# A two-layer decoder in one kernel: keys and values of twelve more items made at the head of the last phase, and two phases in another order of pieces

## The reference, cut to what matters

```
x = x + L0_attn(layernorm(x))            # causal attention over sines and cosines
x = x + L0_xattn(layernorm(x), ctx_768)  # attention to a context of 192 features
x = x + L0_ffn(layernorm(x))             # 16 experts, one per token, fixed capacity
x = x + L1_attn(layernorm(x))            # attention across the batch axis
x = x + L1_xattn(layernorm(x), ctx_768)
x = x + L1_ffn(layernorm(x))             # gated, operands quantised to four bits
```

```
q = einsum('sbd,ed->sbe', x, Wq);  k = einsum('sbd,ed->sbe', x, Wk)
align = softmax(tanh(einsum('sbd,tbd->bst', q, k) / sqrt(256)))
out = einsum('bst,tbd->sbd', align, x)
```

```
q = x @ Wq;  k = ctx @ Wk;  v = ctx @ Wv        # 16 heads of 16 features
out = softmax(q k^T / 4) v;  return out @ Wo
```

## Time and profile before

| | us |
|---|---|
| median of 3 runs | 3186.0 |
| lowest, highest | 3185.05, 3187.09 |
| profiled execution, its own time | 3185.23 |
| span of its trace | 3183.5 |
| TensorE busy | 3009.7 (95%) |
| VectorE busy | 2357.7 (74%) |
| ScalarE busy | 1802.2 (57%) |
| GpSimd busy | 1276.7 (40%) |
| batch attention, projections of steps 1 to 15 | 1813.47 to 1938.63 |
| last phase, first to last query projection | 1964.30 to 3064.42 |

### The profile page before, as it was taken

How to read it: one execution, slowest core, us unless ns; L and a number is a source line. 1 busy time by engine, 2 the same in 40 slices (tenths; PEclk the granted TensorE clock), 3 DMA queues, 4 the chain that set the end, 5 groups by cost and what they waited for, 6 DMA issues and landing times. The chain is left out here.

```text
span 3183.5 us, 57497 instructions
## 1 busy us (share of the span) xinstructions
PE 3009.7 (95%) x21110; PEld 2118.6 (67%) x21110; DVE 2357.7 (74%) x4842; ACT 1802.2 (57%) x3262; POOL 1276.7 (40%) x1927
## 2 busy tenths in 40 slices
PE   5899999999999999899999896799999999999998
PEld 3677777777777767566666563466666777777776
DVE  4799999999999986242111495689899888888886
ACT  5788888888888873111111232456556555555553
POOL 5466666666666652100000352233334333333332
PEclk7999999999999999899999998899999999999999
DMA  8888777778777774533334254534443434433330
GB/s 154 150 116 121 115 108 115 115 115 121 114 107 115 110 101 121 176 124 124 104 103 151 73 179 104 87 64 73 80 83 62 69 59 69 67 61 59 60 50 21
DMA packets 298345, 318.34 MB, mean 100 GB/s; under 512 B 35958, under 2 KB 279526, under 8 KB 298064
## 3 DMA queue, kind: packets, MB, share of 16 engines
q1 hardware_dynamic: 283664, 290.60, 51.1%
q0 software_dynamic: 6144, 15.68, 1.5%
q10 hardware_dynamic: 8256, 8.39, 0.8%
HBM read 104.31 MB, written 58.79 MB: 51 GB/s over the span
## 5 line engine op out<-in xcount | busy, mean ns | idle before, releaser
L629 DVE TENSOR_REDUCE xa_mx<-bank 128x2 f32<-128x512 f32 x1024 | 660.9, 687 | 147.9 <-PE bank L619 145.0
L733 ACT ACTIVATE xa_p<-bank 128x512 f32<-128x512 f32 x1024 | 569.7, 597 | 271.1 <-PE bank L723 268.9
L744 DVE SCALAR_TENSOR_TENSOR xa_p<-xa_p,bank 128x1024 f32<-128x1024 f32 x256 | 301.4, 1217 | 24.2 <-PE bank L712 13.8
L2204 POOL DMA_INDIRECT sa_y<-expert_out,sa_s x64 | 68.2, 1066 | 525.1 <-DMA expert_out<-ex_y 481.6
L756 PE MATMUL bank<-xa_p,xa_v 128*32 128x256 f32 x4096 | 272.9, 391 | 0.3 <-ACT ra_ot L1150 0.3
L1088 ACT ACTIVATE xa_p<-bank 128x384 f32<-128x384 f32 x512 | 235.9, 499 | 65.1 <-PE bank L1076 62.7
L1980 ACT ACTIVATE ex_h<-bank,ex_b 128x512 f32<-128x512 f32 x64 | 44.0, 687 | 362.3 <-PE bank L1969 362.3
L1097 POOL TENSOR_SCALAR_AFFINE_SELECT xa_p<-xa_p 128x256 f32<-128x256 f32 x512 | 199.2, 407 | 83.4 <-ACT xa_p L1088 82.8
L1999 PE MATMUL bank<-ex_w,ex_h 128*128 128x256 f32 x1024 | 224.8, 380 | 1.2 <-issue 0.9
L1969 PE MATMUL bank<-ex_xt,ex_w 128*128 128x512 f32 x512 | 224.0, 596 | 0.7 <-ACT ex_xt L1960 0.7
L619 PE MATMUL bank<-xa_ks,ex_w 96*128 96x256 bf16 x1024 | 197.3, 280 | 17.3 <-DMA ex_w<-xa_pq 14.3
(11 more groups left out here) (308 smaller groups left out, 6774.9 us busy)
## 6 DMA issues: line engine op xcount, KB each, us to landing
ex_w<-ra_parts SPq DMA_DIRECT2D x384, 128.0 KB, 4.6
xa_ks<-xa_pk SPq DMA_DIRECT2D x384, 128.0 KB, 4.6
ex_w<-in_L_ffn_W SPq DMA_DIRECT2D x32, 1024.0 KB, 6.9
xa_qs<-xa_pq SPq DMA_DIRECT2D x192, 128.0 KB, 4.7
ex_w<-xa_pq SPq DMA_DIRECT2D x192, 128.0 KB, 4.5
ra_x<-in_x SPq DMA_DIRECT2D x32, 256.0 KB
xa_ctx<-in_ctx_t SPq DMA_DIRECT2D x64, 128.0 KB, 2.2
queue<-zeros ACTq DMA_DIRECT2D x4, 2048.0 KB, 11.8
```

Of the source, the lines that this page charges most:

```text
L629: c.nc.vector.tensor_reduce(c.xa.row_max[:, :, n], halves(c.banks[2 + n % 2]), AX.X, ALU.max).then_inc(s.max_taken, 1)
L733: c.nc.scalar.activation(c.xa.p_beside[:, n // 2 % 4, :, n % 2, :], halves(c.banks[n % 2]), ACT.Exp, scale=SCALE).then_inc(s.exp, 1)
L744: c.nc.vector.scalar_tensor_tensor(out=p, in0=p, scalar=1.0, in1=c.banks[bank][:, :].unsqueeze(1).broadcast_to([P, TC, 2 * S]), op0=ALU.mi ...
```

## The change

A constant LATE = 12 is added. For items 16 to 27 of the last phase, TensorE makes keys in bank 7 and values in bank 5 in the phase's first four periods (`pe_late_keys`, `pe_late_values`), ScalarE copies both to a `keeps` tile (`act_late_keys`, `act_late_values`), SyncE stores the tile, and the item reads them back as the first sixteen do. The load waits for the store. Only items 28 to 31 still make keys and values in their own periods.

```
-AHEAD = 16
+AHEAD, LATE = 16, 12
 def was_ahead(b):
-    return B <= b < B + AHEAD
+    return B <= b < B + AHEAD + LATE

+def pe_late_keys(c, bank, b):
+    s = c.xa.s
+    c.pe.wait_ge(s.ctx_in[b % 2], 32 * (b // 2 + 1))
+    c.pe.wait_ge(*c.bank_out[bank])
+    side_matmuls(c, bank, c.wx.Wk, c.xa.ctx[b % 2]).then_inc(s.k_made, 1)
+    c.bank_out[bank] = (s.k_copied, b - B + 1)
+def pe_late_values(c, bank, b):
...
+    token_matmuls(c, bank, c.xa.ctx[b % 2], c.wx.Wv).then_inc(s.v_made, 1)
+    c.bank_out[bank] = (s.v_copied, b - B + 1)
+def act_late_keys(c, bank, b):
+    s, par = c.xa.s, b % 2
+    c.act.wait_ge(s.k_made, b + 1)
+    c.act.wait_ge(s.kept_out[par], 16 * ((b - B) // 2))
+    c.nc.scalar.activation(c.xa.keeps[par][:, 0], c.banks[bank][:, :], ACT.Copy).then_inc(s.k_copied, 1)
...
 def sp_xa_kept(c, kept, b):
...
+    c.sp.wait_ge(s.kept_out[par], 16 * ((b - B) // 2 + 1))
     for n in range(2):
         c.nc.sync.dma_start(c.xa.kept[par][n], kept[b - B][:, n]).then_inc(s.kept_in[par], 16)

 def pe_phase_e(c):
...
-        for b, _ in due(n, period, (27,), first=AHEAD):
+        for b in at(n, (401, 403, 745, 873, 961, 1209, 1337, 1394, 1609, 1785, 1817, 1865), B + AHEAD):
+            pe_late_keys(c, 7, b)
+        for b, _ in due(n, period, (216,), first=AHEAD + LATE):
             pe_xa_keys(c, 7, c.wx, B + b)
...
 def phase_e(c, d):
...
+    c.xa.keeps = [c.sb(f"xa1_keep{n}", [P, 2, KC * S]) for n in range(2)]
```

More of the change, by code:

```diff
@@ L2393, in pe_phase_d @@
     pe_d_first_turn(c)
-    for n in range((STEPS_D - 1) * period + 48):
-        for b, k in due(n, period, (27, 28), STEPS_D, first=1):
+    for n in range((STEPS_D - 1) * period + 29):
+        for b, k in due(n, period, (7, 8), STEPS_D, first=1):
             pe_d_turn(c, b, k)
-        for b, k in due(n, period, (30, 31), STEPS_D):
+        for b, k in due(n, period, (11, 12), STEPS_D):
             pe_d_project(c, b, k)
-        for b, _ in due(n, period, (34,), STEPS_D):
+        for b, _ in due(n, period, (15,), STEPS_D):
             pe_d_score(c, b)
-        for b, k in due(n, period, (41, 42, 44, 47), STEPS_D):
+        for b, k in due(n, period, (22, 23, 27, 28), STEPS_D):
             pe_d_sum(c, b, k)
@@ L2439, in pool_phase_d @@
     period = ROUND_D["pool"]
-    for n in range((STEPS_D - 1) * period + 6):
-        for b, _ in due(n, period, (2,), STEPS_D, first=2):
+    for n in range((STEPS_D - 1) * period + 5):
+        for b, _ in due(n, period, (1,), STEPS_D, first=2):
             pool_d_gather(c, d["expert_out"], b)
-        for b, _ in due(n, period, (5,), STEPS_D, first=1):
+        for b, _ in due(n, period, (4,), STEPS_D, first=1):
             pool_d_power(c, b)
@@ L2450, in sp_phase_d @@
     sp_xa_kept(c, d["kept"], B)
-    for n in range((STEPS_D - 1) * period + 10):
-        for b, _ in due(n, period, (0,), STEPS_D):
+    for n in range((STEPS_D - 1) * period + 19):
+        for b, _ in due(n, period, (1,), STEPS_D):
             sp_d_next(c, d, b)
-        for b, _ in due(n, period, (9,), STEPS_D):
+        for b, _ in due(n, period, (18,), STEPS_D):
             sp_d_out(c, out_rows[b], b)
@@ L2762, in pe_phase_e @@
             pe_e_turn_hidden(c, 2 + k % 2, b, k)
-        for b, _ in due(n, period, (299,), B - 1):
+        for b, _ in due(n, period, (2336,), B - 1):
             pe_e_down(c, 7, b)
@@ L2813, in act_phase_e @@
     period = ROUND_E["act"]
-    for n in range((B - 1) * period + 156):
-        for b, _ in due(n, period, (4,), first=1):
+    for n in range((B - 1) * period + 1449):
+        for b in at(n, (305, 355, 537, 641, 689, 809, 913, 969, 1097, 1137, 1145, 1425), B + AHEAD):
+            act_late_keys(c, 7, b)
+        for b in at(n, (353, 354, 593, 625, 713, 865, 897, 961, 1017, 1146, 1185, 1249), B + AHEAD):
+            act_late_values(c, 5, b)
+        for b, _ in due(n, period, (248,), first=1):
@@ L2816, in act_phase_e @@
             act_xa_high_k(c, 7, c.wx, B + b)
-        for b, _ in due(n, period, (6,), first=1):
+        for b, _ in due(n, period, (264,), first=1):
             act_xa_middle_k(c, B + b)
-        for b, _ in due(n, period, (5,)):
+        for b, _ in due(n, period, (240,)):
             act_xa_xn_t(c, 6, B + b)
-        for b, _ in due(n, period, (9,)):
+        for b, _ in due(n, period, (280,)):
             act_xa_high_q(c, 6, c.wx, B + b)
-        for b, _ in due(n, period, (13,)):
+        for b, _ in due(n, period, (304,)):
@@ L2824, in act_phase_e @@
             act_xa_middle_q(c, B + b)
-        for b, _ in due(n, period, (17,), first=1):
+        for b, _ in due(n, period, (352,), first=1):
             act_xa_values(c, 7, B + b)
-        for b, _ in due(n, period, (48,)):
+        for b, _ in due(n, period, (592,)):
             act_xa_rows(c, 2, 1, B + b)
-        for b, k in due(n, period, (54, 55, 56, 57, 58, 59, 60, 61, 63, 64, 66, 67, 68, 69, 70, 71)):
+        for b, k in due(n, period, (640, 648, 656, 664, 680, 688, 696, 704, 712, 720, 736, 744, 752, 760, 768, 776)):
```

153 lines of the change are left out of this document (84 added, 69 removed).

## The result

The changed kernel takes 3137.71 us (median of 4 runs, 3137.54 to 3137.85), the kernel before 3185.99 us (4 runs). The ratio is 0.9848, 95% interval 0.9836 to 0.9861: 48.3 us less, where 44 (3142) were forecast and 3128 to 3162 given.

The account below looks back on a forecast made before the run. TensorE was taken to bound steady periods, waits and lower clock the head, TensorE and VectorE batch attention. Terms -37.6 + 4.0 - 7 - 2 = -42.6 from 3185.23 us gave 3142.6, stated as 3142, range 3128 to 3162.

Parts of the forecast that it names:

- Term 1: Last phase: items 16 to 27 read stored keys and values, saving 3.13 us each, -37.6 us.
- Term 2: Head, items 0 to 4: takes the 24 pieces, 40.3 us of work, mostly in waits; +4.0 us, bounds -5 to +25.
- the clock alone: Head: by the skill's clock rule alone it would run at full clock, making its term about 0.
- Term 3: Batch attention: new order covers the 0.43 us wait, step 8.36 against 8.94 us; -7 us, bounds -9 and +8.
- Rival C: Batch attention is bound by its own store: step 9.5 us, +8 in place of -7, total 3157; 10%.
- Term 4: Steady periods of the last phase: rearranged pieces give -0.1 us each over 23 periods, -2 us; bounds -10 and +8.
- Rival B: The head gives no cover to half of its pieces: +20 in place of +4, total 3158; 14%.
- Rival D: Everything fits: head 0, batch attention -9, no period above its 34.05 us of work (-10), total 3129; 9%.
- Rival E: Last-phase periods: VectorE's and ScalarE's pieces hold each other up, 2 us a period, +54, total 3197; 5%.
- F: Last phase: stored keys don't shorten a period because their loads come late, about 3180; 2%.
- the signs: Markers 34.1 to 34.6 us apart, items 4 to 27; head 120 to 130, clock near 1.00; batch-attention step 8.3 to 8.5.

Follow-up runs that it names:

- e1_d_only: The kernel before with only the five batch-attention functions taken from the changed kernel; 3169.91 us against 3182.54 (ratio 0.9962).
- e2_d_rest: The kernel before with only VectorE's, GpSimd's and SyncE's new order in batch attention; 3180.95 us against 3183.17 (ratio 0.9992).
- e1_late6: The changed kernel with LATE = 6, so only twelve of the 24 pieces are made in the head, for items 16 to 21; 3143.39 us (ratio 0.988).
- e3_early12: The changed kernel with four pieces, for items 16 and 17, made before the barrier and the head's last four places empty; 3136.18 us.

## Why the prediction came out right, and where its steps were off

**Term 1** held. It gave 12 x 3.13 = 37.6 us; after, the two kinds of periods differ by 3.01, and by the paces of before the twelve items account for 37.7 of the 42.0 us between the markers of items 4 and 31. Six items alone gave 18.0 between the same markers.

**Term 2** was +4.0 for the head and nothing for a gate piece and a transposition that move from the tail into it. Measured +3.60 and -1.69, so +1.9 in all; the 1.6 us of those two pieces are right (tail -1.7 with and without late items). The accounting of the 40.3 us of pieces, LATE = 12 in the first trace against LATE = 0: idle time of the head 34.4 to 7.5 us, which takes 26.9; busy time 84.9 to 116.7, 31.7 more for 40.3 of work, so 8.6 come from the clock; the head grows by 4.8. What was off is, first, the pieces in item 0's wait: I had them up to 5 us late if at the lower clock, and they ended 2.3 early, at the full level from the second on. Second, I gave the pieces in running work half of the clock's loss back; two stretches got all of it. All of the growth sits behind the twelfth piece, 3.8 of 4.9 us between items 3 and 4, where six pieces stand in a stretch that had the least idle time. That stretch I had at +0.5, and it grew by 0.4, because the new order had already shortened it from 37.28 (`e1_d_only`) to 33.94 us: two errors that cancelled.

On the clock: where the pieces filled the waits, the granted clock rose to 1.00, stretch by stretch. The section "HAM oscillation" of the Trainium skill (TensorE: Matmul & The Clock Gate) has waits between short bursts of matmuls as what brings the lower clock; the traces agree, with 0.71, 0.84 and 0.95 in the last three stretches with no pieces and 1.00 in each with all. But the clock alone (term about 0) missed the 4.8 us: in the last stretch TensorE is busy 37.70 of 37.71 us, at 1.00, and there is no room for more work.

**Term 3** named the right gain and the wrong mechanism. It took TensorE's busy time of before, 8.36 us a step, as the floor. Gap-free, the same work is busy 112.72 us in `e1_d_only`, 8.05 a step. Most of the rest is the last matmuls of a group, which overlap the next group when that is ready and count in full when a wait follows: in an undisturbed step of before the third sum takes 0.52 us, the turn 0.93 and the fourth sum 0.60, and in `e1_d_only` the turn takes 0.87 and both sums 0.90. And the prediction let the order of TensorE and ScalarE cover the 0.43 us by themselves: alone they cost 23.5 us, since the division of VectorE then sits in a ring with the sum. VectorE's new order, with the earlier add that I had as a side gain, opens the ring; that it is the add and not the rest of VectorE's, GpSimd's and SyncE's order is argued from the rows, since no run moved it alone. That the forecast of -7 fits the first pair (-9.9 there, 2.35 given back ahead of it in unchanged code) is partly luck: on undisturbed steps the same order gives 12.6.

Rival C (the store's landing as a new bound) fell: no wait of VectorE for a store stands in any trace, and SyncE issues gates and store 0.65 us apart in each step:

```profile
1837.94 0.60 SPq L2217 DMA_DIRECT2D sa_g<-gates  x1
1838.59 0.60 SPq L2418 DMA_DIRECT2D x<-sa_out  x1
```

In the earlier trace rows store and loads stood the other way round, and with the new order GpSimd's 28.0 us of waits for gates are gone, and in `e2_d_rest` the long steps with them. I had priced that move only as a risk.

**Term 4** was -2 and came to -4.3 (42.0 less 37.7): 0.13 us in each of the kept periods, 0.26 in the others, while the two waits stay at 0.42 and 0.16 us:

```profile
2336.45 0.73 PE L756 MATMUL bank<-ex_w,xa_ks 99*128 99x256 bf16 x4 [0.42 <-DVE ex_w L2637]
...
2961.01 5.45 PE L622 MATMUL bank<-ff_wd,fe_ht 128*128 128x256 f32 x24 [0.16 <-ACT fe_ht L1911]
```

The difference is in TensorE's busy time (34.05 to 33.90, 37.41 to 37.19), from other neighbours in its row; I have not taken that apart.

**Rival B** (half of the pieces uncovered, +20) fell with the head of `e1_late6` and of the change. **Rival D** had the right size for batch attention but expected the 0.42 us waits to go. **Rival E** fell: VectorE's maxima and ScalarE's exponentials show no new wait in a period. **F** fell: no wait for kept keys.

The sum itself has a small slip: 3142.6 for the profiled execution and 0.8 more for the median make 3143.4, not 3142. Of the signs, the pace (34.34), the head (124.16) and the step (8.36 in the mean) came as written; the clock of the head's first stretch did not, with 0.71.

## What to carry to other kernels

Work that an in-order engine will do anyway is free where that engine waits, and costs its full length elsewhere: with what the items save set against them, the same 24 pieces gave 31 us in the head and cost 5 in steady periods. Fill gaps one by one and look at the marker of each stretch, since the price comes all at once where a stretch has no idle time left. Inside a stretch, look for the moment at which another engine gets the input of its long piece of work: filler ahead of it delays that engine, filler behind it lies under its work, and taking the latter out again can lose the clock and make the stretch longer. When several queues get a new order together, don't credit one queue's move with the gain before it ran alone: a sum moved behind a turn is only a gain if the engine that reads it has moved its own work as well.

## What the runs showed that I had not expected

- A kernel with four pieces less (3.3 us of busy time) in a stretch took 1.7 us longer in it, at a granted clock of 0.91 in place of 1.00 (`e3_early12`).
- Busy time of TensorE was no floor for its work: fourteen steps that counted 117.02 us busy, with waits between, run gap-free in 112.7.
- Unchanged code ahead of batch attention ended between 1799 and 1806 us in different traces; over fourteen steps the same order took 112.7 to 113.6 us in some traces and 116.4 to 117.0 in others. Both are larger than the difference between some of the variants, and only markers separate them.
